# The last chunk of columns in one piece, nine loads through a ring of half rows

## Chip, cores and metric

One core of one Trainium2 chip. The metric is the device time of one execution in microseconds (us); lower is better. Everything is float32.

## What is computed

x is 8192 nodes of 64 features, adj a full 8192 x 8192 matrix, u a random tensor in the shape of x.

```
keep   = (u >= 0.1)
x_drop = x * keep / 0.9
h      = x + adj @ x_drop
out    = (h - mean(h)) / sqrt(var(h) + 1e-5)      # over the 64 features of a node
```

The kernel leaves the factor 1/0.9 for later and centres x and x_drop over the features at the start. The sums are then centred too, so that at the end only the variance is missing.

## The kernel before

**Layout.** The host lays adj out so that each load reads contiguous bytes. The output's 8192 nodes are 16 chunks of 512 columns (`COLS`). For one chunk the sum over the 8192 source nodes runs over 64 blocks (`NB`) of 128. A block of a wide chunk is 128 partitions x 512 columns, 256 KB. Two *rows* of 32 blocks (`SLOTS = 2`, `PB = 32`) make a chunk; one row is 8 MB and stands in DRAM in one piece, 64 KB per partition. The last chunk is cut in two narrow ones of 256 columns (`NARROW = 2`), whose blocks are 128 KB each.

**The ring.** `ring` holds 5 half rows (`RING = 5`, `HALF = 16` blocks, 4 MB each), 20 MB. SyncE issues all loads on one queue (L109 to L170). A whole row is one load of 8 MB into two neighbouring places; every fifth row wraps round the ring's end and is loaded as two halves (`wrapped`, L123). The 30 rows (`ROWS`) of the 15 wide chunks go through it, the last one in two halves (L157, L158). Ahead of a load SyncE waits on `half_used` until TensorE is through with the place (L146, L153). The narrow chunks follow in 11 parts (L31, L159 to L164): 26, 21 and 17 blocks, then 15, 12, 10, 8, 7, 5, 4 and 3 of 128 KB each.

```
PARTS = ((26, 21, 17), (15, 12, 10, 8, 7, 5, 4, 3))
```

**TensorE** (L190 to L253). For each block `products` (L192) multiplies the block by the 64 features of `xdrop`; even blocks fill partitions 0 to 63 of `acc`, odd ones 64 to 127. The trace has two matmul records per block. After a wide chunk ScalarE copies `acc` to `sums_T` (L270), and `fold_rows` (L201) adds the two halves with matmuls by the constant `fold`, which also turns the result so that nodes lie on partitions. VectorE and ScalarE then normalise 512 nodes (`normalise`, L328; `spread`, L259), beside the next chunk. The wide chunks run in a loop of three times five (L210). The first narrow chunk uses a second accumulator, `acc[1]`. Its fold stands behind the first part of the second narrow chunk (L241), together with the *lifting*, in which `x` enters `lifted` through a matmul by 0.9 times the identity (L245), so that the last nodes need no addition later.

**The tail.** Behind the last part ScalarE copies `acc` in two pieces of 128 columns (L284, L285), TensorE folds each into `lifted` (L249, L252), ScalarE squares and sums (L289) and takes the root (L294), VectorE inverts and scales (L351, L353), and SyncE stores the last 256 nodes (L169). All the other nodes are stored in one go (L167) once the first narrow chunk is done (`rows_ready`, `FINAL`).

**The head.** x and u are loaded ahead of row 0 (L111, L112). VectorE masks and centres in four quarters (L315), then centres x in four quarters (L321).

Of the kernel before, what the change touches and what calls it, by code (L numbers as in the profile page):

```python
# [6 lines left out]
D = 64  # L7
P = 128
NB = N // P
# [3 lines left out]
SLOTS = 2  # L13
PB = NB // SLOTS
NARROW = 2
# [4 lines left out]
FINAL = CHUNKS - 2 + NARROW  # L20

RING = 5
HALF = PB // 2
ROWS = (CHUNKS - 1) * SLOTS
# [6 lines left out]
PARTS = ((26, 21, 17), (15, 12, 10, 8, 7, 5, 4, 3))  # L31


def graph_layernorm(nc, x, adj, adj_last, u, out):
# [6 lines left out]
    with ctx:  # L41
# [13 lines left out]
        late_free = sb("late_free", [P, 1])  # L55
# [10 lines left out]
        acc = [pb(f"acc{i}", [P, COLS]) for i in range(2)]  # L66
        folded = pb("folded", [P, J, D])

        lifted = pb("lifted", [P, LAST_J, COLS])

        narrow = ring[:, :, :].rearrange("p b i -> p (b i)").rearrange("p (b i) -> p b i", i=LAST_COLS)

        parts = [(m, sum(sizes[:n]), size) for m, sizes in enumerate(PARTS) for n, size in enumerate(sizes)]
# [5 lines left out]
        late_in = sem("late_in")  # L79
# [4 lines left out]
        narrow_done = sem("narrow_done")  # L84
        sums_copied = sem("sums_copied")
        half_copied = sem("half_copied")
# [22 lines left out]
        @block.sync  # L109
        def _(sp):  # L110
            sp.dma_start(x_sb[:, :, :], x[:, :, :]).then_inc(x_in, 16)  # L111
            sp.dma_start(xdrop[:, :, :], u[:, :, :]).then_inc(u_in, 16)  # L112

            def load(r, w, first, halves, arrived):

                place = (2 * w + first) % RING
                sp.dma_start(ring[:, place * HALF:(place + halves) * HALF, :],  # L117
                             adj[r, :, first * HALF:(first + halves) * HALF, :]).then_inc(arrived, 16)

            def whole(r, w):  # L120
                load(r, w, 0, 2, row_in[w])

            def wrapped(r, w):  # L123

                sp.wait_ge(half_used, r * 2 - (RING - 1))
                load(r, w, 0, 1, row_in[w])
                sp.wait_ge(half_used, r * 2 - (RING - 2))
                load(r, w, 1, 1, wrap_in)

            WRAP = RING // 2  # L130
            whole(0, 0)
            whole(1, 1)
            load(2, WRAP, 0, 1, row_in[WRAP])
            sp.wait_ge(half_used, 1)
            load(2, WRAP, 1, 1, wrap_in)
            for w in range(WRAP + 1, RING):
                sp.wait_ge(half_used, w * 2 - (RING - 2))
                whole(w, w)
            with sp.Fori(1, ROWS // RING - 1) as t:
                for w in range(RING):  # L140
                    r = t * RING + w
                    if w == WRAP:
                        wrapped(r, w)
                    else:

                        sp.wait_ge(half_used, r * 2 - (RING - 2))  # L146
                        whole(r, w)
            for w in range(RING):
                r = ROWS - RING + w
                if w == WRAP:  # L150
                    wrapped(r, w)
                elif w < RING - 1:
                    sp.wait_ge(half_used, r * 2 - (RING - 2))  # L153
                    whole(r, w)
                else:
                    sp.wait_ge(half_used, r * 2 - (RING - 2))
                    load(r, w, 0, 1, row_in[w])  # L157
                    load(r, w, 1, 1, late_in)  # L158
            for n, (m, b, size) in enumerate(parts):  # L159

                end = (m * LAST_PB + b + size - 1) // (2 * HALF)
                sp.wait_ge(half_used, 2 * ROWS - (RING - 1) + end)
                sp.dma_start(narrow[:, m * LAST_PB + b:m * LAST_PB + b + size, :],
                             adj_last[m, :, b:b + size, :]).then_inc(part_in[n], 16)  # L164
# [4 lines left out]
            sp.dma_start(out[:, NB - LAST_J:NB, :], x_sb[:, NB - LAST_J:NB, :]).then_inc(stored, 16)  # L169
            sp.wait_ge(stored, 32)  # L170

        @block.gpsimd
        def _(pool):

            nc.gpsimd.memset(late_free[:, :], 0.0).then_inc(late_in, (ROWS // RING - 1) * 16)
# [15 lines left out]
        def _(pe):  # L191
            def products(i, piece, k0, blocks, cols):  # L192

                for b in range(blocks):
                    k = k0 + b
                    h = k % 2
                    last = nc.tensor.matmul(acc[i][D * h:D * h + D, 0:cols], xdrop[:, k, :], piece[:, b, :],  # L197
                                            start=(k < 2), stop=(k >= NB - 2))
                return last

            def fold_rows(c, nj=J):  # L201

                pe.wait_ge(sums_copied, c + 1)
                for j in range(nj):
                    last = nc.tensor.matmul(folded[:, j, :], sums_T[:, j * P:j * P + P], fold[:, :],  # L205
                                            start=True, stop=True)
                last.then_inc(folded_ready, 1)

            pe.wait_ge(fold_ready, 1)
            with pe.Fori(0, (CHUNKS - 1) // RING) as f:  # L210

                for v in range(RING):
                    for n in range(HALVES):
                        h = v * HALVES + n
                        cycle = f * (HALVES // 2) + h // (2 * RING)
                        w = h % (2 * RING) // 2
                        if h % 2 == 0:
                            pe.wait_ge(row_in[w], cycle * 16 + 16)
                        elif w == RING // 2:
                            pe.wait_ge(wrap_in, cycle * 16 + 16)  # L220
                        elif w == RING - 1:
                            pe.wait_ge(late_in, cycle * 16 + 16)
                        if v == 0:
                            pe.wait_ge(dropped, n + 1)
                        place = h % RING
                        products(0, ring[:, place * HALF:(place + 1) * HALF, :], n * HALF, HALF,
                                 COLS).then_inc(half_used, 1)

                    fold_rows(f * RING + v)

            for m in range(NARROW):
                for n, (of, k0, size) in enumerate(parts):
                    if of != m:
                        continue
                    pe.wait_ge(part_in[n], 16)
                    b = m * LAST_PB + k0
                    last = products(1 - m, narrow[:, b:b + size, :], k0, size, LAST_COLS)
                    if k0 + size == NB:
                        last.then_inc(narrow_done, 1)
                    if m and k0 == 0:  # L240
                        fold_rows(CHUNKS - 1, nj=LAST_J)  # L241

                        pe.wait_ge(lift_ready, 1)
                        pe.wait_ge(x_centred, HALVES)
                        for j in range(LAST_J):  # L245
                            nc.tensor.matmul(lifted[:, j, 0:D], lift[:, :], x_sb[:, NB - LAST_J + j, :],  # L246
                                             start=True, stop=False)
            pe.wait_ge(sums_copied, FINAL + 1)
            nc.tensor.matmul(lifted[:, 0, 0:D], sums_T[:, 0:P], fold[:, :],  # L249
                             start=False, stop=True).then_inc(folded_ready, 1)  # L250
            pe.wait_ge(half_copied, 1)
            nc.tensor.matmul(lifted[:, 1, 0:D], sums_T[:, P:2 * P], fold[:, :],  # L252
                             start=False, stop=True).then_inc(folded_ready, 1)  # L253

        @block.scalar
        def _(act):
# [8 lines left out]
            def wide(c, again=True):  # L265
# [4 lines left out]
                nc.scalar.copy(sums_T[:, :], acc[0][:, :]).then_inc(sums_copied, 1)  # L270
# [6 lines left out]
            act.wait_ge(narrow_done, 1)  # L277
            act.wait_ge(folded_ready, CHUNKS - 1)
            nc.scalar.copy(sums_T[:, 0:LAST_COLS], acc[1][:, 0:LAST_COLS]).then_inc(sums_copied, 1)  # L279
            spread(CHUNKS - 1, LAST_J)  # L280

            act.wait_ge(narrow_done, 2)
            act.wait_ge(folded_ready, FINAL)
            nc.scalar.copy(sums_T[:, 0:P], acc[0][:, 0:P]).then_inc(sums_copied, 1)  # L284
            nc.scalar.copy(sums_T[:, P:2 * P], acc[0][:, P:2 * P]).then_inc(half_copied, 1)  # L285

            for j in range(LAST_J):
                act.wait_ge(folded_ready, FINAL + 1 + j)
# [4 lines left out]
            act.wait_ge(last_var, LAST_J)  # L293
            nc.scalar.activation(std[:, 0:LAST_J], square_sum[:, 0:LAST_J], ACT.Sqrt, bias=eps_lifted[:, :],  # L294
# [3 lines left out]
        def _(dve):  # L298
# [3 lines left out]
            def centre(out, in_, q, which, ready):  # L302
                n = which * HALVES + q + 1
# [11 lines left out]
            for q in range(HALVES):  # L315
# [4 lines left out]
                centre(xdrop, xdrop, q, 0, dropped)  # L320
            for q in range(HALVES):  # L321
                centre(x_sb, x_sb, q, 1, x_centred)
# [57 lines left out]
```

## Time and profile before

| | us |
|---|---|
| median of 3 runs | 642.91 |
| lowest, highest | 642.82, 643.89 |
| the profiled execution's own time | 643.65 |
| its span | 641.9 |
| TensorE busy, share of the span | 78% |
| VectorE, ScalarE | 8%, 3% |
| mean DMA rate over the span | 428 GB/s |

The profile shows one execution. "PE" is TensorE's matmuls, "PEld" its loading of weights, "DVE" VectorE, "ACT" ScalarE, "SPq" SyncE's issuing of DMAs. L197 is line 197 of the kernel. The span runs from the first instruction to the last. 1.75 us of the execution's own time lie outside it.

### The profile page before, as it was taken

The page shows a single profiled execution, that of the slowest core. Times are in us where ns is not written, and L with a number is a line of the kernel's source. Part 1 is how long each engine was busy: PE and PEld are TensorE (multiplying, and loading weights), DVE is VectorE, ACT ScalarE, POOL GpSimd, SP SyncE. Part 2 cuts the span into 40 slices and gives each one's busy share as a digit, 9 for nine tenths or more (in the row PEclk, how much of TensorE's full clock was granted, in tenths as well). Part 3 has the DMA queues.
Part 4 walks back from the last instruction along what each step waited for, and adds up shares of the span by engine and source line. Part 5 has one row for each costly group of instructions (what it writes and reads, how often), then busy time and mean ns, then how long its engine had stood idle before and what let it go on. Part 6 is the DMA issues. An engine that isn't in the chain of part 4 may idle for free.

```text
span 641.9 us, 5108 instructions
## 1 busy us (share of the span) xinstructions
PE 498.1 (78%) x2308; PEld 176.7 (28%) x2308; DVE 53.7 (8%) x102; ACT 17.8 (3%) x41; POOL 1.4 (0%) x12
## 2 busy tenths in 40 slices
PE   0098858888947986959878938977959977959997
PEld 0032313222312232313223312322312322323365
DVE  1930101001010010100001010010100101010001
ACT  0000200000000000000000000000000000000000
POOL 0000000000000000000000000000000000000000
PEclk9998979988979898979979979988988897978999
DMA  9999999999999999999999999999999999999997
GB/s 392 437 412 426 441 441 450 404 442 425 438 441 434 421 449 404 445 453 417 437 441 412 453 417 433 457 417 415 459 421 445 429 429 427 439 417 432 426 422 327
DMA packets 7495, 274.84 MB, mean 428 GB/s; under 512 B 832, under 2 KB 960, under 8 KB 1472
## 3 DMA queue, kind: packets, MB, share of 16 engines
q1 hardware_dynamic: 7488, 274.73, 99.4%
q8 instruction: 7, 0.11, 0.1%
HBM read 272.63 MB, written 2.10 MB: 428 GB/s over the span
## 4 chain that ended last, share of the span: by engine, by line
DMA 63%; PE 35%; ACT 1%; issue 0%; SPq 0%; DVE 0%; ACTq 0%; DVEq 0%
DMA ring<-adj 63%; PE acc L197 34%; PE folded L205 1%; ACT sums_T L270 0%; ACT L270 0%; SPq L117 0%; ACT squares L289 0%; PE lifted L249 0%; PE lifted L246 0%; SPq L112 0%; SPq L111 0%; ACT std L294 0%; DVE x_sb L353 0%; ACT sums_T L284 0%; DVE rstd L351 0%
## 5 line engine op out<-in xcount | busy, mean ns | idle before, releaser
L197 PE MATMUL acc<-ring,xdrop 128*64 128x512 f32 (+1 forms) x2176 | 480.1, 602 | 128.5 <-DMA ring<-adj 128.5
L197 PEld LDWEIGHTS acc<-ring,xdrop 128*64 128x64 f32 x2176 | 160.7, 145 | 435.7 <-issue 286.6
L330 DVE SCALAR_TENSOR_TENSOR y<-folded,x_sb 128x256 f32<-128x256 f32 (+1 forms) x16 | 6.7, 416 | 553.5 <-PE folded L205 553.5
L205 PE MATMUL folded<-fold,sums_T 128*128 128x64 f32 x124 | 17.2, 281 | 11.7 <-ACT sums_T L270 11.7
L270 ACT COPY sums_T<-acc 128x512 f32<-128x512 f32 x15 | 8.8, 586 | 487.4 <-PE acc L197 487.4
L205 PEld LDWEIGHTS folded<-fold,sums_T 128*128 128x128 f32 x124 | 15.0, 191 | 25.3 <-ACT sums_T L270 24.9
L334 DVE TENSOR_TENSOR squares<-y 128x256 f32<-128x256 f32 (+1 forms) x16 | 6.7, 416 | 0.6
L341 DVE TENSOR_TENSOR x_sb<-y,rstd 128x256 f32 (+1 forms) x16 | 6.7, 416 | 0.6
L337 DVE TENSOR_REDUCE square_sum<-squares 128x4 f32<-128x256 f32 (+1 forms) x16 | 6.6, 412 | 0.5
L316 DVE SCALAR_TENSOR_TENSOR xdrop<-xdrop,x_sb 128x1024 f32<-128x1024 f32 x4 | 4.9, 1219 | 13.4 <-DMA xdrop<-u 13.4
L262 ACT ACTIVATE std<-square_sum,eps 128x4 f32<-128x4 f32 (+1 forms) x16 | 4.8, 297 | 43.6 <-DVE square_sum L337 43.6
L308 DVE SCALAR_TENSOR_TENSOR x_sb<-node_sum,x_sb 128x1024 f32<-128x1024 f32 x4 | 4.9, 1225 | 0.1
L308 DVE SCALAR_TENSOR_TENSOR xdrop<-node_sum,xdrop 128x1024 f32<-128x1024 f32 x4 | 4.9, 1225 | 0.1
L304 DVE TENSOR_REDUCE node_sum<-xdrop 128x16 f32<-128x1024 f32 x4 | 4.9, 1220 | 0.1
L304 DVE TENSOR_REDUCE node_sum<-x_sb 128x16 f32<-128x1024 f32 x4 | 4.8, 1211 | 0.0
L339 DVE RECIPROCAL rstd<-std 128x4 f32<-128x4 f32 (+1 forms) x16 | 2.8, 177 | 5.8 <-ACT std L262 5.8
L270 ACT ACT_TABLE_LOAD x1 | 1.3, 1283 | 67.8 <-PE acc L197 67.8
L262 ACT ACT_TABLE_LOAD x1 | 1.3, 1283 | 0.0
L351 DVE RECIPROCAL rstd<-std 128x2 f32<-128x2 f32 x1 | 0.2, 165 | 11.4 <-ACT std L294 11.4
L249 PE MATMUL lifted<-fold,sums_T 128*128 128x64 f32 x2 | 0.4, 299 | 0.4 <-ACT sums_T L284 0.4
L279 ACT COPY sums_T<-acc 128x256 f32<-128x256 f32 x1 | 0.4, 372 | 12.2 <-PE acc L197 12.2
L246 PE MATMUL lifted<-x_sb,lift 128*128 128x64 f32 x4 | 0.6, 275 | 0.0
(22 smaller groups left out, 5.3 us busy)
## 6 DMA issues: line engine op xcount, KB each, us to landing
ring<-adj SPq DMA_DIRECT2D x14, 4096.0 KB, 32.1
ring<-adj_last SPq DMA_DIRECT2D x1, 3328.0 KB, 35.4
ring<-adj_last SPq DMA_DIRECT2D x1, 2688.0 KB, 24.2
ring<-adj_last SPq DMA_DIRECT2D x1, 2176.0 KB, 29.0
x_sb<-x SPq DMA_DIRECT2D x1, 2048.0 KB, 7.7
xdrop<-u SPq DMA_DIRECT2D x1, 2048.0 KB, 12.1
out<-x_sb SPq DMA_DIRECT2D x1, 1984.0 KB, 11.8
ring<-adj_last SPq DMA_DIRECT2D x1, 1920.0 KB, 27.1
```

What stands on the lines that cost most here:

```text
L197: last = nc.tensor.matmul(acc[i][D * h:D * h + D, 0:cols], xdrop[:, k, :], piece[:, b, :], start=(k < 2), stop=(k >= NB - 2))
L205: last = nc.tensor.matmul(folded[:, j, :], sums_T[:, j * P:j * P + P], fold[:, :], start=True, stop=True)
L262: nc.scalar.activation(std[:, 0:nj], square_sum[:, 0:nj], ACT.Sqrt, bias=eps[:, :], scale=1.0 / D).then_inc(std_ready, 1)
L270: nc.scalar.copy(sums_T[:, :], acc[0][:, :]).then_inc(sums_copied, 1)
L304: nc.vector.reduce_sum(node_sum[:, which, quarter(q)], in_[:, quarter(q), :], AX_X).then_inc(node_sum_ready, 1)
L308: nc.vector.scalar_tensor_tensor(out=out[:, quarter(q), :], in0=sums, scalar=-1.0 / D, in1=in_[:, quarter(q), :], op0=ALU.mult, op1=ALU.ad ...
L316: nc.vector.scalar_tensor_tensor(out=xdrop[:, quarter(q), :], in0=xdrop[:, quarter(q), :], scalar=P_DROP, in1=x_sb[:, quarter(q), :], op0= ...
L330: nc.vector.scalar_tensor_tensor(out=y[:, 0:nj, :], in0=folded[:, 0:nj, :], scalar=1.0 / KEEP, in1=x_sb[:, bass.ds(block0, nj), :], op0=AL ...
L334: nc.vector.tensor_tensor(squares[:, 0:nj, :], y[:, 0:nj, :], y[:, 0:nj, :], ALU.mult).then_inc(squares_ready, 1)
L337: nc.vector.reduce_sum(square_sum[:, 0:nj], squares[:, 0:nj, :], AX_X).then_inc(var_ready, 1)
L339: nc.vector.reciprocal(rstd[:, 0:nj], std[:, 0:nj]).then_inc(rstd_ready, 1)
L341: nc.vector.tensor_tensor(x_sb[:, bass.ds(block0, nj), :], y[:, 0:nj, :], per_row(rstd, nj), ALU.mult).then_inc(rows_ready, 1)
```

## The change

1. The last chunk is no longer cut in two. It keeps 512 columns and comes in nine parts of 17, 13, 10, 8, 6, 4, 3, 2 and 1 wide blocks (256 KB each).
2. Both rows of a chunk stand together in DRAM, so a partition's row there is 128 KB (`SLOTS = 1`, `PB = 64`). The ring's half stays at 16 blocks (`HALF = PB // 4`). A load of a whole or half row takes 64 or 32 KB of every 128 KB.
3. The last but one wide row (28) is loaded in halves, the last one (29) in quarters, and TensorE waits for each.
4. SyncE's loads are written out rather than looped over. On TensorE the last five wide chunks are written out.
5. One accumulator instead of two. The narrow chunk's own copy, fold and normalising go.
6. The lifting covers four blocks of nodes and stands first in TensorE's program. For that VectorE centres the last quarter of x first.
7. The tail has four copies, four folds and four squares, and scales and stores 512 nodes. The other nodes are stored once chunk 14 is done.

```diff
-SLOTS = 2
+SLOTS = 1
 PB = NB // SLOTS
-NARROW = 2
+NARROW = 1
...
-FINAL = CHUNKS - 2 + NARROW
+FINAL = CHUNKS - 1
...
-HALF = PB // 2
-ROWS = (CHUNKS - 1) * SLOTS
+HALF = PB // 4
+QUARTER = HALF // 2
+ROWS = (CHUNKS - 1) * 2
...
-PARTS = ((26, 21, 17), (15, 12, 10, 8, 7, 5, 4, 3))
+PARTS = (17, 13, 10, 8, 6, 4, 3, 2, 1)
...
+            def load(r, half, blocks, arrived, first=0):
+                h = 2 * r + half
+                if h >= RING:
+
+                    sp.wait_ge(half_used, h + blocks // (HALF + 1) - (RING - 1))
+                place = h % RING * HALF + first
+                b = h % HALVES * HALF + first
+                sp.dma_start(ring[:, place:place + blocks, :], adj[h // HALVES, :, b:b + blocks, :]).then_inc(arrived, 16)
+
+            for r in range(ROWS):
+                w = r % RING
+                if w == RING // 2:
+                    load(r, 0, HALF, row_in[w])
+                    load(r, 1, HALF, wrap_in)
+                elif r < ROWS - 2:
+                    load(r, 0, 2 * HALF, row_in[w])
+                elif r < ROWS - 1:
+
+                    load(r, 0, HALF, row_in[w])
+                    load(r, 1, HALF, late_in[0])
                 else:
...
+                    load(r, 0, QUARTER, row_in[w])
+                    for n in range(1, 4):
+                        load(r, n // 2, QUARTER, late_in[n], first=n % 2 * QUARTER)
+            for n, (b, size) in enumerate(parts):
+
+                sp.wait_ge(half_used, 2 * ROWS - (RING - 1) + (b + size - 1) // HALF)
+                sp.dma_start(ring[:, b:b + size, :], adj_last[0, :, b:b + size, :]).then_inc(part_in[n], 16)
 
             sp.wait_ge(rows_ready, FINAL)
-            sp.dma_start(out[:, 0:NB - LAST_J, :], x_sb[:, 0:NB - LAST_J, :]).then_inc(stored, 16)
+            sp.dma_start(out[:, 0:NB - J, :], x_sb[:, 0:NB - J, :]).then_inc(stored, 16)
...
+            pe.wait_ge(lift_ready, 1)
+            pe.wait_ge(x_centred, 1)
+            for j in range(J):
+                nc.tensor.matmul(lifted[:, j, 0:D], lift[:, :], x_sb[:, NB - J + j, :], start=True, stop=False)
             pe.wait_ge(fold_ready, 1)
-            with pe.Fori(0, (CHUNKS - 1) // RING) as f:
+            with pe.Fori(0, (CHUNKS - 1) // RING - 1) as f:
...
+            for n, (b, size) in enumerate(parts):
+                pe.wait_ge(part_in[n], 16)
+                last = products(ring[:, b:b + size, :], b, size)
+            last.then_inc(last_done, 1)
+            for j in range(J):
+                pe.wait_ge(last_copied, j + 1)
+                nc.tensor.matmul(lifted[:, j, 0:D], sums_T[:, j * P:j * P + P], fold[:, :],
+                                 start=False, stop=True).then_inc(last_folded, 1)
```

## Rows read from the trace of the kernel before

**Rows 1.** The page, part 3: DMA queues, their packets, MB and share of 16 engines.
```profile
q1 hardware_dynamic: 7488, 274.73, 99.4%
q8 instruction: 7, 0.11, 0.1%
```

**Rows 2.** Chain of waits in order of time, from 547 us: start, us, what.
```profile
547.67 28.63 DMA ring<-adj
...
607.08 1.10 PE folded L205 x8
608.18 17.41 PE acc L197 x158
625.60 0.59 PE folded L205 x4
626.18 0.45 PE lifted L246 x4
626.63 10.95 PE acc L197 x98
637.58 0.02 issue
```

**Rows 3.** Issues of SyncE: second half of row 27, both halves of row 29, last part.
```profile
L117 SPq DMA_DIRECT2D ring<-adj x1: 328/328/328, 525.3 to 525.3; - x1
...
DMA to landing us min/median/max: 31.6/31.6/31.6
...
L117 SPq DMA_DIRECT2D ring<-adj x2: 328/380/432, 561.4 to 561.8; - x2
...
DMA to landing us min/median/max: 24.6/29.3/34.0
...
L163 SPq DMA_DIRECT2D ring<-adj_last x1: 9052/9052/9052, 601.8 to 601.8; - x1
...
DMA to landing us min/median/max: 33.2/33.2/33.2
```

**Rows 4.** TensorE in order of time behind rests; last row: stretch 570.90 to 581.10.
```profile
130.89 15.47 PE L197 MATMUL acc<-ring,xdrop 128*64 128x512 f32 x64 [5.40 <-DMA ring<-adj]
...
324.57 15.91 PE L197 MATMUL acc<-ring,xdrop 128*64 128x512 f32 x64 [5.39 <-DMA ring<-adj]
...
479.52 16.93 PE L197 MATMUL acc<-ring,xdrop 128*64 128x512 f32 x64 [7.45 <-DMA ring<-adj]
...
518.22 13.95 PE L197 MATMUL acc<-ring,xdrop 128*64 128x512 f32 x64 [3.70 <-DMA ring<-adj]
...
576.35 30.04 PE L197 MATMUL acc<-ring,xdrop 128*64 128x512 f32 x128 [6.33 <-DMA ring<-adj]
...
570.90:581.10 10.20, 4.75 (x12) 1.46 (x14) 1.18 (x4) 0.30 (x1) 0.00 (x0) 0.50 0.97 418
```
(The columns of that last row are the stretch, its length, busy time and count of PE, PEld, DVE, ACT and POOL, granted clock, DMA share and GB/s.)

**Rows 5.** Timeline: start, us, engine, line, operation, [idle before]; one scaling at 610, then the tail.
```profile
610.25 0.42 DVE L341 TENSOR_TENSOR x_sb<-y,rstd 128x256 f32 x1
...
637.60 0.27 ACT L284 COPY sums_T<-acc 128x128 f32<-128x128 f32 x1 [10.11 <-PE acc L197]
...
638.39 0.22 ACT L289 ACTIVATE squares<-lifted 128x64 f32<-128x64 f32 x1 [0.36 <-PE lifted L249]
...
639.62 0.29 DVE L353 TENSOR_TENSOR x_sb<-lifted,rstd 128x128 f32<-128x128 f32 x1
639.94 0.34 SPq L169 DMA_DIRECT2D out<-x_sb  x1
```

**Rows 6.** DMA issues: count, KB each, median us to landing; the big store was issued at 628.04.
```profile
out<-x_sb SPq DMA_DIRECT2D x1, 1984.0 KB, 11.8
...
out<-x_sb SPq DMA_DIRECT2D x1, 64.0 KB, 1.5
```

**Rows 7.** VectorE's centring of x (four, 29.3 to 36.4), and TensorE's first matmuls.
```profile
L308 DVE SCALAR_TENSOR_TENSOR x_sb<-node_sum,x_sb x4: 1224/1225/1226, 29.3 to 36.4; 128x1024 f32<-128x1024 f32 x4
...
32.72 16.76 PE L197 MATMUL acc<-ring,xdrop 128*64 128x512 f32 x64 [32.72 <-DMA ring<-adj]
```

**Rows 8.** Stretch 608.20 to 635.00, columns as in the last row of rows 4.
```profile
608.20:635.00 26.80, 26.80 (x244) 17.93 (x246) 3.20 (x10) 0.96 (x3) 0.00 (x0) 1.00 1.01 422
```

More of the change, by code:

```diff
@@ L65, in graph_layernorm @@
         rstd = sb("rstd", [P, J])
-        acc = [pb(f"acc{i}", [P, COLS]) for i in range(2)]
+        acc = pb("acc", [P, COLS])
         folded = pb("folded", [P, J, D])
-        lifted = pb("lifted", [P, LAST_J, COLS])
-        narrow = ring[:, :, :].rearrange("p b i -> p (b i)").rearrange("p (b i) -> p b i", i=LAST_COLS)
-        parts = [(m, sum(sizes[:n]), size) for m, sizes in enumerate(PARTS) for n, size in enumerate(sizes)]
+        lifted = pb("lifted", [P, J, COLS])
+        parts = [(sum(PARTS[:n]), size) for n, size in enumerate(PARTS)]
         row_in = [sem(f"row_in{w}") for w in range(RING)]
         wrap_in = sem("wrap_in")
-        late_in = sem("late_in")
+        late_in = [sem(f"late_in{n}") for n in range(4)]
         part_in = [sem(f"part_in{n}") for n in range(len(parts))]
@@ L112, in _ @@
             sp.dma_start(xdrop[:, :, :], u[:, :, :]).then_inc(u_in, 16)
[L114 to L154, printed above, removed]
-                else:
[L156 to L164, printed above, removed]
+            def load(r, half, blocks, arrived, first=0):
[5 more added lines that the diff above has]
+                sp.dma_start(ring[:, place:place + blocks, :], adj[h // HALVES, :, b:b + blocks, :]).then_inc(arrived, 16)
@@ L191, in _, with products @@
         def _(pe):
-            def products(i, piece, k0, blocks, cols):
+            def products(piece, k0, blocks):
                 for b in range(blocks):
@@ L196, in products, with fold_rows @@
                     h = k % 2
-                    last = nc.tensor.matmul(acc[i][D * h:D * h + D, 0:cols], xdrop[:, k, :], piece[:, b, :],
+                    last = nc.tensor.matmul(acc[D * h:D * h + D, :], xdrop[:, k, :], piece[:, b, :],
                                             start=(k < 2), stop=(k >= NB - 2))
                 return last
-            def fold_rows(c, nj=J):
+            def fold_rows(c):
                 pe.wait_ge(sums_copied, c + 1)
-                for j in range(nj):
+                for j in range(J):
                     last = nc.tensor.matmul(folded[:, j, :], sums_T[:, j * P:j * P + P], fold[:, :],
@@ L214, in _ @@
                         h = v * HALVES + n
[L215 to L222, printed above, removed]
                         if v == 0:
@@ L224, in _ @@
                             pe.wait_ge(dropped, n + 1)
-                        place = h % RING
-                        products(0, ring[:, place * HALF:(place + 1) * HALF, :], n * HALF, HALF,
-                                 COLS).then_inc(half_used, 1)
+                        whole_half(h, f * (HALVES // 2) + h // (2 * RING)).then_inc(half_used, 1)
                     fold_rows(f * RING + v)
-            for m in range(NARROW):
-                for n, (of, k0, size) in enumerate(parts):
-                    if of != m:
-                        continue
[L235 to L253, printed above, removed]
+            for c in range(CHUNKS - 1 - RING, CHUNKS - 1):
+                for n in range(HALVES):
+                    h = c * HALVES + n
+                    r = h // 2
+                    if r == ROWS - 2 and n % 2:
+                        pe.wait_ge(late_in[0], 16)
+                    if r < ROWS - 1:
+                        whole_half(h, r // RING).then_inc(half_used, 1)
+                        continue
+                    for e in range(2):
+                        quarter = n % 2 * 2 + e
+                        if quarter:
+                            pe.wait_ge(late_in[quarter], 16)
+                        else:
+                            pe.wait_ge(row_in[RING - 1], ROWS // RING * 16)
+                        b = h % RING * HALF + e * QUARTER
+                        last = products(ring[:, b:b + QUARTER, :], n * HALF + e * QUARTER, QUARTER)
+                    last.then_inc(half_used, 1)
+                fold_rows(c)
@@ L269, in wide @@
                     act.wait_ge(folded_ready, c)
-                nc.scalar.copy(sums_T[:, :], acc[0][:, :]).then_inc(sums_copied, 1)
+                nc.scalar.copy(sums_T[:, :], acc[:, :]).then_inc(sums_copied, 1)
                 spread(c)
@@ L275, in _ @@
                 wide(c)
[L277 to L282, printed above, removed]
+            act.wait_ge(last_done, 1)
             act.wait_ge(folded_ready, FINAL)
[L284 to L288, printed above, removed]
+            for j in range(J):
+                nc.scalar.copy(sums_T[:, j * P:j * P + P], acc[:, j * P:j * P + P]).then_inc(last_copied, 1)
+            for j in range(J):
+                act.wait_ge(last_folded, j + 1)
                 nc.scalar.activation(squares[:, j, :], lifted[:, j, 0:D], ACT.Square,
@@ L300, in quarter, with centre @@
                 return slice(q * HALF, q * HALF + HALF)
-            def centre(out, in_, q, which, ready):
-                n = which * HALVES + q + 1
+            def centre(out, in_, q, n, which, ready):
                 nc.vector.reduce_sum(node_sum[:, which, quarter(q)], in_[:, quarter(q), :],
@@ L319, in _ @@
                 dve.wait_ge(masked, q + 1)
-                centre(xdrop, xdrop, q, 0, dropped)
-            for q in range(HALVES):
-                centre(x_sb, x_sb, q, 1, x_centred)
+                centre(xdrop, xdrop, q, q + 1, 0, dropped)
+            for n, q in enumerate((HALVES - 1, *range(HALVES - 1))):
+                centre(x_sb, x_sb, q, HALVES + n + 1, 1, x_centred)
             dve.wait_ge(x_centred, HALVES)
```

27 lines of the change are left out of this document (17 added, 10 removed).

## Prediction, made before the change was run

> **What bounds the kernel now.** I began with the page. The load queue took 99.4% of the time of its 16 DMA engines [rows 1], while TensorE rests ahead of nearly every row: the matrix streams in without a pause, and the span is that stream plus what follows its last byte. Equal work done later or earlier inside the stream is worth nothing, so everything turns on the last 80 us.
>
> The chain of waits, in order of time, shows who ends last there [rows 2]. It follows the loads until 576.3 us (547.67 + 28.63), where row 28 lands as one piece of 8 MB. From there on it never touches a DMA again: TensorE works on four half rows (30.04, [rows 4]), then come the fold of chunk 14 (1.10), the first narrow piece (17.41), its fold and the lifting of x (0.59 + 0.45) and the second narrow piece (10.95), to 637.58.
>
> The issues of SyncE give the other side [rows 3]: an issue's start plus its time to landing. Row 29 lands in halves at 586.0 and 595.8, the last narrow part at 601.8 + 33.2 = 635.0. Its three narrow blocks would be 6 matmuls of 10.95/98 = 0.11, 0.67 us. So TensorE could have ended at 635.7 and ended at 637.6: it was **1.9 us behind the stream**, because it sat idle 6.33 us until 576.35 and then ran at a granted clock of 0.50 until 581.1 [rows 4], which is 1.2 of its 2.4 GHz. A stretch of 64 matmuls takes 13.95 at the full clock, and 15.47 to 16.93 behind a long rest [rows 4]: such a rest costs 1.5 to 3.0 us.
>
> After 637.58 comes the tail: copies, folds, squares, root, scaling, and the last store issued at 639.94 [rows 5], landed 1.5 later [rows 6]. The big store landed at 628.0 + 11.8 = 639.8 [rows 6], 4.8 after the last load, which is 2 MB at the stream's rate. It was thus served behind all loads, though issued 7 us before the last of them landed.
>
> **The change, part by part.** *Row 28 in halves, row 29 in quarters.* The first half of row 28 (4 MB) is there some 9.7 us before 576.3, at 566.6, while TensorE works on chunk 13 until 568.2 and folds it until 570.0 (576.35 less the rest of 6.33, [rows 4]; the fold and its copy take 1.8 of that). The rest of 6.33 us goes. Half rows take 6.98 each (13.95/2): half 56 runs 570.0 to 577.0, half 57 to 584.0, the quarters (landing at 581.2, 586.0, 590.9, 595.9; 3.5 each) to 587.5, 591.0, 594.5 and 599.4, waiting 1.4 us for the last. With copy and fold (0.6 + 1.1 + 0.1 of hand-overs) TensorE stands ready at 601.2.
>
> *Loads after that.* The last 16 MB took 595.8 to 635.0, that is 39.2 us, 0.61 per wide block (256 KB). The nine parts land at about 606.3, 614.2, 620.4, 625.3, 629.0, 631.4, 633.2, 634.5 and 635.1. The 0.1 in that last number is for one load more in all (49 for 48). From below a load more costs 0, from above 0.1: row 29 in two halves took 19.5 (576.3 to 595.8), the whole row 28 took 19.4 (556.9 to 576.3) [rows 2, 3]. I take the upper end.
>
> *TensorE on the parts.* A wide block costs 13.95/32 = 0.436. Work left after part n landed, added to its landing: part 0 gives 606.3 + 64 x 0.436 = 634.2; part 3 635.8; part 4 629.0 + 16 x 0.436 = 636.0; part 5 635.8; part 8 635.5. But 601.2 to 606.3 is a new rest of 5.1 us. Rests of 5.40 and 5.39 cost 1.5 and 2.0 (15.47 and 15.91), one of 3.70 nothing [rows 4]. With the mean of 1.75 part 0 gives 635.95, just under 636.0. So TensorE ends at **636.0**, 1.55 sooner. The two folds and the lifting that stood between the narrow pieces (1.04 us) are inside this: the lifting goes to the head, where TensorE rests until row 0 lands at 32.7. Its cover: VectorE's first centring of x begins at 29.3 and takes 1.2, and TensorE's first matmul on row 0 starts at 32.72 [rows 7], so four liftings (1.1 us, by the fold's row of 8 matmuls) end at 31.7. If that cover went, 1 us late at the head would be made good by the next rests.
>
> *Tail.* Four copies of 128 columns for two, four folds and four squares for two. A copy takes 0.27, a square 0.22 [rows 5], a fold 1.10/4 = 0.275 [rows 2], and the three overlap along the line. The slowest sets the pace: two folds more are 0.55, and I add 0.05 for ScalarE, which copies before it squares. The last scaling is 256 elements for 128: 0.13 by the 0.42 and 0.29 of this product at both widths [rows 5]. Then the last store is 128 KB for 64: 0.15, between 0 and 0.3 (twice its own bytes' time at the stream's rate). Together +0.9. From both sides 0.6 to 1.2.
>
> *Stores and queues.* The big store now waits for chunk 14 alone and is issued 20 us sooner, but it stands behind the parts in the same queue. It lands at 635.1 + 4.7 = 639.8, as before. The last store would be issued at 639.94 - 1.55 + 0.75 = 639.1 and land at 640.8, 1.0 after the big one, so that is no floor yet. SyncE's loops become straight code: nothing waits on it, as it issues 24.6 to 34.0 us ahead of landing [rows 3]. *Instructions.* TensorE's five last wide chunks are written out; the page counts 7 fetches in 0.11 MB, 0.016 MB each [rows 1]. Some four more cost the stream 0.07 MB, 0.15 us if spread evenly; I take 0 to 1, and 0.1.
>
> **Sum:** -1.55 + 0.9 + 0.1 = -0.55 on the profiled execution, whose own time is 643.65 (span 641.9): 643.1. That execution lies 0.74 above the median of 642.91. Its rest at 576 cost 30.04 - 27.90 = 2.1 where such rests cost 1.5 to 3.0, so executions differ by this at the very place which ends last; the runs from 642.82 to 643.89 fit. The new order is ruled by landings and gains less on a lucky execution. Between 643.1 and 642.91 - 0.55 = 642.4 I take **642.7**.
>
> **Weighed against a rule.** The last five parts carry 16 wide blocks, 4 MB, in pieces of 1.5 MB to 256 KB. The stretch 608.2 to 635.0, all small parts down to 384 KB, ran at 422 GB/s [rows 8], row 28 at 8.39 MB in 19.4 us, 432. The Trainium skill, "DMA: Bandwidth & Descriptors", section Bandwidth, advises loads of at least 1 MiB for 75% of peak. The trace disagrees for loads queued behind one another; by that rule the 2.5 MB of the last four parts would take some 2 us more.
>
> **Rivals.**
> - *The saving in full.* If the 0.74 is not the clock but something outside the tail, the small parts' landings let TensorE end at 635.6 (1.95 sooner) and the tail grows by its lower end of 0.6, it is 642.91 - 1.95 + 0.6 = 641.6, with nothing for the fetches. For it: only three runs stand behind my reading. Chance 0.20.
> - *Slower by the clock.* The rest before part 0 costs as much as the worst, 3.0. It decides above 1.8 (636.0 - 606.3 - 27.9), to which one of the two rests of 5.4 came: TensorE ends at 637.2 and the tail is 0.9 longer, so 643.65 + 0.6 = 644.2. For it: 5.1 is long enough for a drop. Against: to lengthen the whole by 1.3 it takes the worst rest seen, which was 7.45 long. Chance 0.12.
> - *Slower by the rows in DRAM.* A partition's rows stand 128 KB apart and each wide load takes half of one, where it took a contiguous 8 MB. If each piece of 64 KB takes 1% longer, the 622 us of loading give +6: 649. It decides from 0.3%. Against: half rows already read 32 KB of every 64, at 9.7 to 9.8 per 4 MB, where a whole row takes 19.4 per 8 [rows 2, 3]. The Trainium skill, same page, section Latency and other measured facts, has a pitch of 512 KiB 3% under full rate; it has none of 128 KB, and no run yet shows one; 3% would be some 19 us. Chance 0.08.
> - *It does not do what it says.* TensorE stays behind the stream to the end (the early half finds it late, or a fold waits): only the longer tail remains, 643.65 + 0.9 at most, 643.8 to 644.5. Chance 0.07.
> - *The small loads don't overlap.* A store that stands alone takes 1.5 us to land [rows 6]. If each of the last four parts added a third of that to the stream, it is +2.0: 644.7. Against: the 27 us of [rows 8]. Chance 0.03.
>
> **Numbers.** The forecast has 0.50; its own range is 642.0 to 643.5. Over 0.2%, 1.3 us, can be told from no change here. Faster than 641.6 is most of the first rival and a little of the forecast, 0.20; slower than 644.2 takes the pitch, the small loads and half of the clock and the fourth, with what I can't name, 0.20; the same 0.60. Leaving out the pitch and the outer half of the first rival, the range is 641.4 to 644.3.
>
> **What would show it.** Right: TensorE's rest of 6.33 before 576 gone; row 29's last quarter landing near 595.9; one new rest of about 5 us ahead of part 0, clock 0.50 behind it; TensorE idle a little before each late part and ending 0.9 after the last landing; four copies; the last store issued at about 639.1. Wrong: the row-by-row landings (19.4 per 8 MB) stretched; the last part later than 635.5; TensorE without rests from part 0 to the end; a store ahead of parts.

## The result and the profile after

The changed kernel takes 644.89 us (median of 10, 644.61 to 645.54), the kernel before 643.31 (median of 10, 642.82 to 643.89). The ratio is 1.0023, with a 95% interval of 1.0015 to 1.0030: slower, by 1.6 us. I had forecast no measurable change at 642.7, and 644.89 lies outside the range.

The page of the changed kernel, its head and DMA queues (as rows 1):

```profile
span 642.9 us, 4763 instructions
...
q1 hardware_dynamic: 7632, 274.73, 99.2%
q8 instruction: 12, 0.20, 0.1%
HBM read 272.63 MB, written 2.10 MB: 427 GB/s over the span
```

The same bytes, 144 packets more on q1, and on q8 **12 fetches of instructions for 7**. The span is 1.0 us longer than in [rows 2]'s execution. The chain of waits in order of time shows who ends last:

```profile
534.62 33.20 DMA ring<-adj
...
575.00 32.85 DMA ring<-adj_last
607.85 0.04 issue
607.89 29.96 PE acc L173 x128
637.85 0.02 issue
637.87 0.77 ACT sums_T L265 x4
638.64 0.02 issue
638.66 0.99 ACT squares L269 x8
...
640.28 0.42 DVE x_sb L332
```

The chain leaves the DMA only at the first part; I had TensorE waiting a little for the late parts too. That first part lands at 607.85, where I had 606.3, and TensorE ends at 637.85, 0.3 us later than before instead of 1.55 sooner. From there to the end of the span it is 5.05 us, where it was 4.32: the longer tail.

TensorE in order of time, with the rest before each group (as rows 4):

```profile
567.87 7.09 PE L173 MATMUL acc<-ring,xdrop 128*64 128x512 f32 x32 [0.39 <-DMA ring<-adj]
577.72 18.84 PE L173 MATMUL acc<-ring,xdrop 128*64 128x512 f32 x80 [2.76 <-DMA ring<-adj]
597.30 3.65 PE L173 MATMUL acc<-ring,xdrop 128*64 128x512 f32 x16 [0.74 <-DMA ring<-adj]
601.64 1.10 PE L181 MATMUL folded<-fold,sums_T 128*128 128x64 f32 x8 [0.69 <-ACT sums_T L255]
607.89 29.94 PE L173 MATMUL acc<-ring,xdrop 128*64 128x512 f32 x128 [5.15 <-DMA ring<-adj_last]
```

The rest of 6.33 us before 576 is gone. The new rest before the first part is there too, 5.15 us for 5.1 forecast, and the granted clock behind it is 0.50 (1.2 GHz), as this stretch of the run shows (columns as in rows 4):

```profile
604.60:611.40 6.80, 3.51 (x10) 1.03 (x12) 0.60 (x2) 0.00 (x0) 0.00 (x0) 0.50 0.98 418
```

The last part's issue and its landing (as rows 3), with the issue of the 8-block part above it:

```profile
L142 SPq DMA_DIRECT2D ring<-adj_last x1: 432/432/432, 586.7 to 586.7; - x1
...
DMA to landing us min/median/max: 39.9/39.9/39.9
...
L142 SPq DMA_DIRECT2D ring<-adj_last x1: 5657/5657/5657, 595.0 to 595.0; - x1
...
DMA to landing us min/median/max: 41.5/41.5/41.5
```

They land at 626.6 and 636.5; I had 625.3 and 635.1. A load counts as landed when the last of the 16 DMA engines has reported. The trace records each report, so the first and the last engine can be told apart. For the last load:

```
kernel          first engine   last engine   spread
before             633.28        635.05       1.77
changed            633.24        636.51       3.27
```

The first engine is as early as before, so the stream as such is not slower. The last engine is 1.5 us later. This is what the experiments had to explain, beside the rest with its clock, the rows in DRAM and the tail.

### The profile page after: what moved, and what is told of

Read it like the earlier page. It is cut to its first block, busy times and chain, and to the rows that moved or that the text cites. A ratio compares the mean times of both kernels' runs of the same rounds, so it can differ in the third digit from the quotient of the medians.

```text
span 642.9 us, 4763 instructions
## 1 busy us (share of the span) xinstructions
PE 504.9 (79%) x2184; PEld 170.8 (27%) x2184; DVE 52.5 (8%) x97; ACT 17.9 (3%) x45; POOL 1.3 (0%) x11
## 4 chain that ended last, share of the span: by engine, by line
DMA 65%; PE 33%; ACT 1%; another core or an unknown queue 0%; issue 0%; SPq 0%; DVE 0%; ACTq 0%
DMA ring<-adj 59%; PE acc L173 33%; DMA ring<-adj_last 5%; PE folded L181 0%; ACT L255 0%; ACT sums_T L255 0%; ACT squares L269 0%; ACT sums_T L265 0%; SPq L112 0%; DVE x_sb L332 0%; SPq L111 0%; ACT std L274 0%; DVE rstd L330 0%; ACTq L273 0%
## 5 line engine op out<-in xcount | busy, mean ns | idle before, releaser
L173 PE MATMUL acc<-ring,xdrop 128*64 128x512 f32 x2048 | 485.2, 635 | 91.6 <-DMA ring<-adj 86.3
L173 PEld LDWEIGHTS acc<-ring,xdrop 128*64 128x64 f32 x2048 | 153.3, 146 | 411.4 <-issue 313.1
L310 DVE SCALAR_TENSOR_TENSOR y<-folded,x_sb 128x256 f32<-128x256 f32 x15 | 6.4, 425 | 532.3 <-PE folded L181 532.3
L199 PE MATMUL lifted<-x_sb,lift 128*128 128x64 f32 x8 | 1.9, 424 | 30.9 <-DVE x_sb L287 30.9
L199 PEld LDWEIGHTS lifted<-x_sb,lift 128*128 128x128 f32 x8 | 1.8, 328 | 30.9 <-issue 30.9
L314 DVE TENSOR_TENSOR squares<-y 128x256 f32<-128x256 f32 x15 | 6.4, 425 | 0.5
L321 DVE TENSOR_TENSOR x_sb<-y,rstd 128x256 f32 x15 | 6.4, 424 | 0.5
L317 DVE TENSOR_REDUCE square_sum<-squares 128x4 f32<-128x256 f32 x15 | 6.3, 420 | 0.5
L247 ACT ACTIVATE std<-square_sum,eps 128x4 f32<-128x4 f32 x15 | 4.5, 297 | 39.2 <-DVE square_sum L317 39.2
L319 DVE RECIPROCAL rstd<-std 128x4 f32<-128x4 f32 x15 | 2.7, 178 | 5.5 <-ACT std L247 5.5
L330 DVE RECIPROCAL rstd<-std 128x4 f32<-128x4 f32 x1 | 0.2, 178 | 34.8 <-ACT std L274 34.8
```

The costliest lines, as they stand in the source:

```text
L173: last = nc.tensor.matmul(acc[D * h:D * h + D, :], xdrop[:, k, :], piece[:, b, :], start=(k < 2), stop=(k >= NB - 2))
L247: nc.scalar.activation(std[:, 0:nj], square_sum[:, 0:nj], ACT.Sqrt, bias=eps[:, :], scale=1.0 / D).then_inc(std_ready, 1)
L310: nc.vector.scalar_tensor_tensor(out=y[:, 0:nj, :], in0=folded[:, 0:nj, :], scalar=1.0 / KEEP, in1=x_sb[:, bass.ds(block0, nj), :], op0=AL ...
L314: nc.vector.tensor_tensor(squares[:, 0:nj, :], y[:, 0:nj, :], y[:, 0:nj, :], ALU.mult).then_inc(squares_ready, 1)
L317: nc.vector.reduce_sum(square_sum[:, 0:nj], squares[:, 0:nj, :], AX_X).then_inc(var_ready, 1)
L321: nc.vector.tensor_tensor(x_sb[:, bass.ds(block0, nj), :], y[:, 0:nj, :], per_row(rstd, nj), ALU.mult).then_inc(rows_ready, 1)
```

## Experiments

Three theories. **Fetches:** TensorE's written-out code is fetched by the DMA engines that carry the data, and every load waits for the most delayed one. **Clock:** the rest before the first part sets TensorE's end. **DRAM:** the 128 KB rows are slower. Each comparison has its own runs of the kernel before on the same chip, whose medians went from 642.93 to 643.58.

### e1_loop: the changed kernel with TensorE's loop restored

```diff
-            with pe.Fori(0, (CHUNKS - 1) // RING - 1) as f:
+            with pe.Fori(0, (CHUNKS - 1) // RING) as f:
...
+                        if w == RING - 2 and h % 2:
+                            pe.wait_ge(late_in[0], cycle * 16 + 16)
...
+                                pe.wait_ge(late_in[quarter], cycle * 16 + 16)
...
-            for c in range(CHUNKS - 1 - RING, CHUNKS - 1):
```

GpSimd counts the late semaphores up at the start, as `late_in` was before, so that the waits pass in the loop's first rounds.

> The changed kernel with all 15 wide chunks in TensorE's loop again (three times five); the loads, parts and tail stay as changed. Fetch theory: written-out code is fetched over the same DMA engines, 12 fetches where the kernel before had 7, and a load lands only with its slowest engine. Then 7 or 8 fetches are left, the first part lands at 606.4 to 606.8 instead of 607.9, the last at 635.2 to 635.5 instead of 636.5, and the time falls by 1.0 to 1.4 us against the changed kernel, to about 643.6. Rivals (the clock after the rest before the first part; the rows in DRAM; the longer tail alone): the landings stay where they are and the time stays within 0.3 us of 644.9.

Measured: 643.47 us, ratio to before 0.9999 (0.9990 to 1.0008). The page's row of fetches:

```profile
q8 instruction: 6, 0.10, 0.1%
```

The chain of waits, start, us, what:

```profile
576.07 30.46 DMA ring<-adj_last
606.53 0.04 issue
606.58 30.15 PE acc L176 x128
636.72 0.02 issue
```

The last part's issue and its landing:

```profile
L143 SPq DMA_DIRECT2D ring<-adj_last x1: 7127/7127/7127, 592.5 to 592.5; - x1
...
DMA to landing us min/median/max: 42.9/42.9/42.9
```

Six fetches; the first part lands at 606.5, the last at 635.4, TensorE ends 1.1 us sooner than in the changed kernel and the median falls by 1.4 (1.1 between the two profiled executions). The loads, the parts, the tail and the rest before the first part (4.87 us) are the same or nearly so, and SyncE's loads are still written out: nearly the whole loss is TensorE's written-out code. The time also equals that of the kernel before, so the rest of the change, taken together, is worth nothing.

### e2_rows_64k: the changed kernel with 64 KB rows in DRAM

```diff
-                b = h % HALVES * HALF + first
-                sp.dma_start(ring[:, place:place + blocks, :], adj[h // HALVES, :, b:b + blocks, :]).then_inc(arrived, 16)
+                b = h % 2 * HALF + first
+                sp.dma_start(ring[:, place:place + blocks, :], adj[h // 2, :, b:b + blocks, :]).then_inc(arrived, 16)
```

> The changed kernel with the wide rows laid out as before, 64 KB per partition and a whole row in one piece of 8 MB. DRAM theory: the pitch of 128 KB made the pieces slower; the whole rows land faster and the time falls by over 0.5 us. Fetch theory and clock theory: the first DMA engine's landings are already the same in both kernels, so nothing moves: 644.9 within 0.3.

Measured: 644.82 us, ratio 1.0022 (1.0013 to 1.0031), the changed kernel's own, with 11 fetches ahead of the last load and that load landing at 636.53. The DRAM theory falls. It ran in the same rounds as e1_loop, which is 1.35 us below it.

### e3_before_unrolled and e9_unrolled_again: the kernel before with five chunks written out

```diff
-            with pe.Fori(0, (CHUNKS - 1) // RING) as f:
...
+            with pe.Fori(0, LOOPS) as f:
                 for v in range(RING):
...
+                    chunk(v, f)
+            for f in range(LOOPS, (CHUNKS - 1) // RING):
+                for v in range(RING):
+                    chunk(v, f)
```

`LOOPS` is 2 and `chunk` is the loop's old body.

> The kernel before with the last five wide chunks of TensorE written out, nothing else. Fetch theory: five fetches more, row 28 lands 1.0 to 1.4 us later than 576.3, TensorE, which works without a rest from there on, ends as much later, and the time is 644.3 to 644.7 where the kernel before has 643.3. Rivals (code is free; the clock, DRAM or tail did it): 643.3 within 0.3.

Measured: 645.51 us, ratio 1.0029 (1.0017 to 1.0041). The page's row of fetches:

```profile
q8 instruction: 13, 0.21, 0.1%
```

The chain of waits:

```profile
544.72 32.99 DMA ring<-adj
577.70 0.04 issue
577.75 29.15 PE acc L198 x128
...
627.11 10.95 PE acc L198 x98
638.06 0.02 issue
```

Row 28 lands at 577.7, 1.4 later than the 576.3 of [rows 2], as expected. Written-out code alone makes this kernel slower. The median moved by more than I expected, 1.9 where the landing moved by 1.4. The profiled execution (644.14) was the lowest of six. So I ran the kernel again:

> e3_before_unrolled once more, for a second profile: its first profiled execution (644.14) was the lowest of six, 1.4 us below their median. By the sizes of rests seen so far (1.2 to 3.0 us lost behind a rest) the difference is the clock after the rest of 10 us before row 28: then this profile has row 28 landing near 577.7 again and, if its time is near 645.5, the 128 matmuls behind it taking 30.3 to 30.9 instead of 29.1. Rival (the fetches hit other DMA engines in other executions): row 28 lands later than 578.5.

Measured: 644.22 us (8 runs), ratio 1.0022 (1.0010 to 1.0034), profile at 644.19. Row 28 landed at 577.85 and the 128 matmuls behind it took 29.02. The eight times fall in two groups, 644.1 to 644.2 (five) and 645.2 to 645.8 (three). The kernel before has two as well beside it: 642.6 to 643.0 (six) and 644.0 to 644.3 (three). Group against group the code costs 1.3 to 1.4 us. In its other 63 runs, though, the kernel before shows no such gap: their times fill the range from 642.6 to 644.4. No profile of this kernel fell in the upper group, so that the clock makes the difference was not shown for it. It fits the kernel before: its profiled execution, 643.65, took 30.04 for the same 128 matmuls [rows 4], 1.0 more than here.

### e7_before_all_unrolled: all fifteen chunks written out

```diff
-            with pe.Fori(0, (CHUNKS - 1) // RING) as f:
...
+            for f in range(LOOPS, (CHUNKS - 1) // RING):
                 for v in range(RING):
...
+                    chunk(v, f)
```

`LOOPS` is 0 here.

> The kernel before with all fifteen wide chunks of TensorE written out, no loop: the suspected cost once more. Fetch theory: some 17 to 20 fetches where the kernel before had 7 and e3_before_unrolled 13, hitting the same DMA engines again; row 28 and all later loads land another 0.5 to 2 us later than in e3_before_unrolled, time 645.5 to 647.5. Rival (a one-time cost of leaving the loop): as e3_before_unrolled, 645.5 or less.

Measured: 645.36 us (645.11 to 646.03), ratio 1.0030 (1.0018 to 1.0042). The median lies just under the expected 645.5 to 647.5 and no higher than e3's first one. The page's row of fetches:

```profile
q8 instruction: 18, 0.29, 0.2%
```

The last part's issue and landing:

```profile
L164 SPq DMA_DIRECT2D ring<-adj_last x1: 8711/8711/8711, 603.7 to 603.7; - x1
...
DMA to landing us min/median/max: 34.2/34.2/34.2
```

The last part lands at 637.9, 2.9 later than before. Here are the reports of the 16 engines for that last load, for all eleven kernels; "fetches" are those begun ahead of the first report:

```
kernel                       fetches   first    last    spread
e1_loop                         6      633.36   635.37   2.01
e6_loop_first_part_cut          6      633.28   635.16   1.88
before                          7      633.28   635.05   1.77
e4_row28_halves                 7      633.00   635.26   2.26
e8_row28_halves_finer_end       7      633.31   635.30   1.99
changed                        11      633.24   636.51   3.27
e2_rows_64k                    11      633.35   636.53   3.18
e5_first_part_cut              11      633.40   636.42   3.02
e3_before_unrolled             12      633.25   636.42   3.17
e9_unrolled_again              12      633.13   636.62   3.49
e7_before_all_unrolled         17      633.20   637.90   4.70
```

The spread goes in steps: about 2 up to 7 fetches, 3.0 to 3.5 for 11 or 12, 4.7 for 17. The same steps stand inside each single execution, load by load. Here are the loads on both sides of each step (landing, fetches begun before it, spread):

```
kernel                     landing   fetches   spread
e3_before_unrolled          52.11       0       0.74
                            62.98       1       1.88
                           537.54       8       1.85
                           548.63       9       3.23
changed                    537.95       8       2.33
                           548.39       9       3.05
e9_unrolled_again          537.58       8       1.99
                           548.77       9       3.46
e7_before_all_unrolled     344.01       8       2.02
                           354.96       9       3.27
                           616.88      16       3.55
                           622.88      17       4.96
```

The first, the ninth and the seventeenth fetch make a step, wherever in the execution they fall (the ninth at 542 us in three kernels, at 348 in e7). A step is 0.4 to 1.5 us high, and the fetch behind it can add to it: in e2 the ninth raises the spread from 1.81 to 2.65 and the tenth to 3.24. That is what comes out if the fetches go round the same 8 of the 16 engines: the ninth is the first to meet an engine that is already late, the seventeenth the first to meet one for the third time. For e7's last load, 8 engines report within 0.9 us of the first, six are 2.8 to 3.5 late and two are 4.7 late; two fetches, at 620.7 and 635.7, had come after the sixteenth. The number of late engines is a rougher sign: the kernel before has 7 late for its last load, after 7 fetches, but 7 or 8 for many earlier ones, after 5. The trace's record of a fetch does not name its engine, so the round of 8 is inferred.

Why e7's time is not higher than e3's: e3's median lies among its upper times. The profiles compare better. At row 28 both kernels have the same spread, 3.5 in e7 and in e9, and the third step came only with the fetch at 620.7. From there on e7's loads land late enough to bind: the last one lands at 637.90 and TensorE ends at 639.0, against 638.1 in e9, and the profiled executions differ by as much, 645.12 and 644.19.

### e5_first_part_cut and e6_loop_first_part_cut: the rest before the first part

```diff
-PARTS = (17, 13, 10, 8, 6, 4, 3, 2, 1)
+PARTS = (7, 10, 13, 10, 8, 6, 4, 3, 2, 1)
```

e5 makes this edit in the changed kernel, e6 in e1_loop.

> The changed kernel with its first part of 17 blocks cut into 7 and 10 (ten parts in all), nothing else. Clock theory: TensorE's rest of 5.15 us before the first part shrinks to under 1 us, the clock stays at its upper level, the 30 us of its last run shorten by about 2 us, and then the landings bind: last part 636.5, TensorE's end 637.0 to 637.3 instead of 637.8, time 644.1 to 644.4. Rival (the rest costs nothing, the landings bind already): 644.9 within 0.2.

> Both repairs: the loop of e1_loop and the first part cut into 7 and 10. Fetch and clock theory together: last part at about 635.4, TensorE ends at 635.9 to 636.2 instead of 636.7, time 642.7 to 643.0. If only one of them counts, it stays at e1_loop's 643.5. The longer tail (0.75 us) stays, so it should not reach e4_row28_halves' 642.4.

Measured: e5 645.00 us, ratio 1.0025 (1.0015 to 1.0036); e6 643.63, ratio 1.0007 (0.9998 to 1.0016), where e1_loop has 643.47. e5's clock theory and e6's forecast both missed; e5's rival (644.9 within 0.2) held. In e5, though, the clock fell again, behind the rest of 3.24 us that had moved there, so e5 alone decides nothing (columns as in rows 4):

```profile
616.10:619.40 3.30, 3.30 (x12) 0.86 (x10) 0.00 (x0) 0.00 (x0) 0.00 (x0) 0.50 0.97 416
```

In e6 it stayed at 1.00 to TensorE's end:

```profile
606.40:636.40 30.00, 26.18 (x114) 8.05 (x114) 0.00 (x0) 0.00 (x0) 0.00 (x0) 1.00 1.00 422
```

Yet TensorE ended at 636.5 in e6, only 0.2 sooner than in e1_loop, and the last loads had landed 0.2 sooner too. So the clock theory falls. (Three of e6's eleven times stand apart, 644.8 to 645.2; no profile caught one, and they are not explained.) TensorE in e6:

```profile
595.99 3.65 PE L176 MATMUL acc<-ring,xdrop 128*64 128x512 f32 x16 [1.24 <-DMA ring<-adj]
...
601.36 3.65 PE L176 MATMUL acc<-ring,xdrop 128*64 128x512 f32 x14
606.37 4.51 PE L176 MATMUL acc<-ring,xdrop 128*64 128x512 f32 x20 [1.36 <-DMA ring<-adj_last]
614.29 10.62 PE L176 MATMUL acc<-ring,xdrop 128*64 128x512 f32 x46 [3.41 <-DMA ring<-adj_last]
625.28 11.22 PE L176 MATMUL acc<-ring,xdrop 128*64 128x512 f32 x48 [0.38 <-DMA ring<-adj_last]
```

The rest did not go; it moved to 610.9 to 614.3. TensorE waits once more at 625.28, for the part of 8 blocks, and the 24 blocks left take 11.22 us, 0.468 each, where I had reckoned 0.436. What takes the time is the very end. The last quarter of row 29 (8 blocks, x16) takes 3.65 us, and so does the part of 7 blocks (x14): **an odd block left over costs as much as a pair**. The single records show why. A block's two matmuls start 0.43 us apart, and beside them run the two of a neighbouring block. In the last 2 us of e1_loop the matmuls start in two strings:

```
first string     634.78   635.26   635.69   636.12
second string    634.45   634.88   635.31   635.74
```

The first string starts when the part of two blocks (61 and 62) has landed, at 634.73. Its four matmuls fit the odd blocks 61 and 63, one behind the other; even and odd blocks write different halves of `acc`. That the odd blocks are this string is inferred from the order and the landing. From that landing to the end of TensorE it is the same time in four kernels, whatever the clock did before:

```
kernel                    part of two landed    TensorE ended   between
changed                        635.86              637.84        1.98
e2_rows_64k                    635.88              637.86        1.98
e1_loop                        634.73              636.71        1.98
e6_loop_first_part_cut         634.53              636.50        1.97
e5_first_part_cut              635.78              638.02        2.24
```

I had reckoned 3 x 0.436 = 1.31. Only e5 ended later than this, after its low clock at 616. In the changed kernel the chain through the first part, with 2 us lost to the clock, came to the part of 6 blocks at 630.3, just as that part landed (630.28); from there the landings rule. A last part that holds one even and one odd block should save part of this. No run tried it with wide blocks; e8 below ends so with narrow ones.

### e4_row28_halves: only row 28 in halves, in the kernel before

`split_in` is a new semaphore, counted up at the start like `late_in`:

```diff
+                elif w < RING - 1:
+                    sp.wait_ge(half_used, r * 2 - (RING - 1))
+                    load(r, w, 0, 1, row_in[w])
+                    sp.wait_ge(half_used, r * 2 - (RING - 2))
+                    load(r, w, 1, 1, split_in)
...
+                        elif w == RING - 2:
+                            pe.wait_ge(split_in, cycle * 16 + 16)
```

> The kernel before with row 28 loaded in two halves, nothing else: the half of the change that my prediction counted as the gain, without the longer tail and without more code. If TensorE's lateness of 1.9 us behind the stream comes from the rest before 576 and its clock, the rest goes, TensorE ends at 635.9 to 636.2 instead of 637.6, and the time is 641.6 to 642.0. Rival: the rest only moves on to the next load, or another rest lowers the clock; then 643.3 within 0.4.

Measured: **642.39 us, ratio 0.9983** (0.9974 to 0.9992), faster than both kernels. TensorE in order of time:

```profile
568.83 7.09 PE L204 MATMUL acc<-ring,xdrop 128*64 128x512 f32 x32
576.58 7.09 PE L204 MATMUL acc<-ring,xdrop 128*64 128x512 f32 x32 [0.66 <-DMA ring<-adj]
586.29 8.72 PE L204 MATMUL acc<-ring,xdrop 128*64 128x512 f32 x32 [2.62 <-DMA ring<-adj]
596.02 7.09 PE L204 MATMUL acc<-ring,xdrop 128*64 128x512 f32 x32 [1.00 <-DMA ring<-adj]
```

Further on, the second narrow piece, 49 blocks of it:

```profile
624.74 11.64 PE L204 MATMUL acc<-ring,xdrop 128*64 128x256 f32 x98
```

The rest of 6.33 us becomes rests of 0.66, 2.62 and 1.00, TensorE ends at 636.4 (624.74 + 11.64) instead of 637.6, and the tail stays short. The half row behind the rest of 2.62 still took 8.72 for 7.09 (granted clock 0.50 from 586.2 to 589.6), but that is made good before the end. The gain is 1.2 us where I expected 1.3 to 1.7, so the time just misses the range. TensorE ended 1.12 after the last landing (635.26), where three narrow blocks had been reckoned at 0.67: they too are two odd blocks and an even one. The kernel before was therefore some 1.4 us behind the stream, not 1.9. The times now lie within 642.25 to 642.83, where the kernel before in the same rounds has 642.56 to 644.44.

### e8_row28_halves_finer_end: e4 with smaller last parts

```diff
-PARTS = ((26, 21, 17), (15, 12, 10, 8, 7, 5, 4, 3))
+PARTS = ((26, 21, 17), (15, 12, 10, 8, 6, 5, 4, 2, 2))
```

> e4_row28_halves with the second narrow piece's parts 15, 12, 10, 8, 6, 5, 4, 2, 2 instead of 15, 12, 10, 8, 7, 5, 4, 3. TensorE ended 0.4 us later there than the last landing alone asks for. If the late parts' sizes do that, it ends 0.2 to 0.4 sooner, 642.0 to 642.3; if a further load costs as much as it saves, 642.4 within 0.2.

Measured: 642.27 us, ratio 0.9979 (0.9970 to 0.9988). TensorE ended at 636.04 in its profile, 0.3 sooner, and 0.74 after the last landing (635.30) where e4 has 1.12: its last part is one even and one odd block. Its interval overlaps that of e4, so this step alone isn't settled. It has the lowest median here.

## Why the prediction was wrong

- **What bounds the kernel.** Right, and e4 showed it by itself: TensorE's lateness behind the stream came from row 28 landing in one piece. The lateness was about 1.4 us, not 1.9 (e4).
- **Row 28 in halves, row 29 in quarters.** Right. TensorE was ready for the first part at 602.7, against 601.2. The last quarter landed at 597.2 for 595.9, which is 1.3 of the 1.5 us between.
- **Instructions.** This is the step that failed: "Some four more cost the stream 0.07 MB, 0.15 us if spread evenly; I take 0 to 1, and 0.1." The fetches were five more and are not spread evenly. They made the most delayed engine 1.0 to 1.3 us later than in e1_loop, which lacks them, and with it every landing from row 28 on; e1_loop's median is 1.4 us lower. I had the number of fetches in the page and priced their bytes, not the waiting of all 16 engines for one.
- **Loads after that.** Without the fetches 606.5 and 635.4 in e1_loop, against 606.3 and 635.1: right within 0.3.
- **TensorE on the parts.** The second step that failed. I gave every block 0.436, but that is half a pair. The last parts of two and one blocks leave two odd blocks one behind the other, 1.98 us from the landing of the part of two for the 1.31 reckoned. With that landing 0.2 later than forecast, TensorE would have ended at 636.7 (e1_loop), not 636.0.
- **Tail.** +0.73 by the two spans, against +0.9; within its bounds. The head's lifting took 1.94 us instead of 1.1 and ended at 32.8, just before row 0 landed; it and the early big store cost nothing seen.
- **Sum.** With 1.1 us at TensorE's end for the fetches (637.8 less 636.7) and 0.7 for the parts, the forecast of -1.55 there becomes +0.25 (measured +0.27); with +0.73 for the tail the span is 1.0 longer. The profiled executions differ by as much, 644.67 and 643.65. The medians differ by 1.6, because the profiled execution of before lay 0.3 above its median, in the direction I had noted, and that of the changed kernel 0.2 below.
- **The rule on small loads.** "DMA: Bandwidth & Descriptors", section Bandwidth, of the Trainium skill asks for 1 MiB a load. In e1_loop the last four parts, 1 MB down to 256 KB, stood among nine that landed from 606.5 to 635.4, 47 blocks behind the first, 12.3 MB in 28.9 us, 426 GB/s. The trace disagrees with the rule for queued loads.
- **Rivals.** The clock's loss at the first part was 2.0, above the 1.8 I gave as deciding, but e6, which lost nothing, shows that it didn't decide. The rows in DRAM cost nothing (e2), so 128 KB is a pitch at which the loss that the same page's section Latency and other measured facts has for 512 KiB does not show.

## What to carry to other kernels

In a kernel bound by its stream of loads, code counts as a load: here the written-out chunks were fetched over the engines that bring the data, and every load landed with the most delayed one. Five fetches cost 1.3 to 1.4 us of 643. Look at the count of fetches before unrolling, and price what the slowest engine does to each landing, not the bytes. When the end of a stream is tuned, take one part of it at a time: here the half that helped (row 28 in halves) was worth 1.2 us on its own and was buried under longer code (1.1 at TensorE's end), a longer tail (0.7) and small last parts with an odd block left over. And price the last blocks by how they run side by side, not by a mean.

## What I had not expected of the hardware

The step in the spread: up to 7 fetches left the last engine about 2 us behind the first, 11 or 12 left it 3.0 to 3.5, 17 left it 4.7, while the first engine's last report stayed within 633.0 to 633.4 in all these kernels. The steps come with the ninth fetch and again with the seventeenth, whenever these fall. The fetches' times (56 to 204 us, then none while the loop repeats, then again with the code behind it) show that this loop of five chunks was fetched once for its three rounds. And 7 blocks take TensorE as long as 8, 3.65 us (e6).
